# One megakernel, first part reshaped: the state-space rows of batch 0 spread by TensorE, the first feed-forward on ScalarE's Silu, and batch 1's scans ordered behind it

## What is computed

```
x += tanh(g_xattn[0]) * ssm(ctx, z=layernorm(x))      # state space, 512 channels, 16 states
x += tanh(g_ffn[0])   * ffn(layernorm(x))             # 512 -> 2048 -> 512, quantized weights
x += tanh(g_xattn[1]) * attention(layernorm(x), ctx)  # 16 heads of 128, keys/values from ctx
x += tanh(g_ffn[1])   * experts(layernorm(x))         # 4 experts

ssm:  u = silu(conv4(in_proj @ ctx) + conv_b);  dt, B, C = x_proj @ u     # 16 + 16 + 16 rows
      delta = softplus(dt_proj @ dt + dt_b)
      state[n] = exp(delta * A[n]) * state[n] + delta * u * B[n]          # for 16 states n
      y = sum_n state[n] * C[n] + D * u;   out = y * silu(z)
ffn:  bit_linear(silu(bit_linear(x, gate)) * bit_linear(x, val), out)
      # rows of x rounded to 8 bits by their maximum, weights to -1, 0, 1 by their mean
```

## Time and profile before

| what | value |
|---|---|
| time, median of 3 runs | 1866.79 us (1866.64 to 1868.19) |
| span of the profiled execution | 1867.3 us |
| TensorE busy | 1758.7 us (94%) |
| VectorE busy | 1317.8 us (71%) |
| ScalarE busy | 955.9 us (51%) |
| GpSimd busy | 663.5 us (36%) |

### The profile page before, as it was taken

One profiled execution on the slowest core, in us unless ns is written; L12 is line 12 of the kernel. 1 busy time (PEld: TensorE's weight loads), 2 busy tenths in 40 slices (PEclk: granted clock), 3 DMA queues, 4 the chain that ended last, 5 costly groups with the idle time before them and its releaser, 6 DMA issues.

```text
span 1867.3 us, 19387 instructions
## 1 busy us (share of the span) xinstructions
PE 1758.7 (94%) x6054; PEld 801.7 (43%) x6054; DVE 1317.8 (71%) x1919; ACT 955.9 (51%) x1904; POOL 663.5 (36%) x693
## 2 busy tenths in 40 slices
PE   8878769989999999999999999999999899999999
PEld 2323233434444344444444544444444344454543
DVE  3978877998998799889887989987643444422221
ACT  6867875656563555575456565564435233330100
POOL 1324522345472244456432464562123333310100
PEclk9989889999999899999999999999999999999999
DMA  8999933688771146697312589841112799846110
GB/s 267 260 289 291 300 109 98 173 211 215 189 195 46 48 102 155 160 266 196 102 31 70 129 199 234 212 109 62 41 47 78 215 301 256 246 141 241 68 51 28
DMA packets 163173, 300.30 MB, mean 161 GB/s; under 512 B 18936, under 2 KB 51704, under 8 KB 160128
## 3 DMA queue, kind: packets, MB, share of 16 engines
q1 hardware_dynamic: 145792, 236.14, 40.3%
q0 software_dynamic: 17280, 62.92, 17.5%
HBM read 177.64 MB, written 58.33 MB: 126 GB/s over the span
## 4 chain that ended last, share of the span: by engine, by line
PE 62%; DVE 18%; issue 6%; ACT 5%; DMA 5%; POOL 2%; SPq 2%; DVEq 0%; ACTq 0%; POOLq 0%
PE p L799 9%; PE p L776 8%; PE p L759 8%; PE p L810 8%; PE p L846 6%; DVE s_M L963 5%; PE p L652 4%; PE p L782 4%; PE p L861 3%; DVE s_M L958 2%; PE p L699 2%; DVE s_M L968 2%; PE p L733 2%; DMA s_bc<-bc_scratch 1%; PE p L738 1%
## 5 line engine op out<-in xcount | busy, mean ns | idle before, releaser
L963 DVE TENSOR_TENSOR_SCAN s_M<-s_M 128x1024 f32<-128x1024 f32 x128 | 296.8, 2319 | 7.8 <-ACT s_M L1218 5.3
L1106 DVE CUSTOM_DVE_ANT_0 s_U<-p,s_U 128x512 f32<-128x512 f32 x256 | 187.3, 745 | 162.8 <-PE p L776 161.5
L776 PE MATMUL p<-s_U 128*128 128x512 f32 x512 | 269.3, 614 | 5.6 <-DVE s_U L1106 2.8
L759 PE MATMUL p<-s_U 128*128 128x512 f32 x512 | 253.7, 604 | 4.7 <-DMA s_U<-in_Wq 2.1
L1445 POOL DMA_DIRECT2D s_u<-s_M x120 | 112.6, 938 | 391.5 <-DVE s_M L968 368.8
L1490 POOL TENSOR_SCALAR s_U<-s_U 128x512 f32<-128x512 f32 x256 | 229.4, 917 | 6.3
L810 PE MATMUL p<-s_U 128*128 128x512 f32 x512 | 224.0, 593 | 0.0
L799 PE MATMUL p<-s_U 128*128 128x512 f32 x472 | 213.6, 593 | 2.6 <-ACT s_U L1348 2.5
L1348 ACT COPY s_U<-p 128x512 f32<-128x512 f32 x196 | 105.3, 592 | 189.7 <-PE p L782 188.4
L1218 ACT ACTIVATE s_M<-s_dl,s_small 128x511 f32<-128x511 f32 x256 | 170.3, 718 | 40.3 <-DVE s_M L963 36.8
L1343 ACT ACTIVATE s_U<-s_U 128x512 f32<-128x512 f32 x256 | 181.6, 710 | 5.3
(11 more groups left out here) (171 smaller groups left out, 2364.3 us busy)
## 6 DMA issues: line engine op xcount, KB each, us to landing
s_u<-s_M POOLq DMA_DIRECT2D x120, 512.0 KB, 7.6
s_bc<-bc_scratch SPq DMA_DIRECT2D x128, 256.0 KB, 5.0
k_scratch<-s_U SPq DMA_DIRECT2D x16, 1024.0 KB, 9.4
v_scratch<-s_U SPq DMA_DIRECT2D x16, 1024.0 KB, 7.8
s_U<-in_Wq SPq DMA_DIRECT2D x64, 256.0 KB, 6.9
s_U<-k_scratch SPq DMA_DIRECT2D x64, 256.0 KB, 5.2
s_U<-rk_scratch SPq DMA_DIRECT2D x64, 256.0 KB, 5.5
s_U<-in_Wo SPq DMA_DIRECT2D x64, 256.0 KB, 4.5
```

Source lines behind the costliest of these rows:

```text
L759: ins = e.matmul(banks[bk][:], wqq[j % 2][:, k, :], axT[b % 2][:, k, :], start=(k == 0), stop=(k == 3))
L776: e.matmul(banks[bk][:], qT[j % 3][:, k * 128:(k + 1) * 128], kT[j % 2], start=True, stop=True).then_inc(S["a_s"], 1)
L963: e.tensor_tensor_scan(w, dA[i % 2], w, 0.0, ALU.mult, ALU.add).then_inc(S["m_s"], 1)
L1106: e.tensor_tensor_reduce(out=Pm[j % 2][:, k, :], in0=banks[ABANK[kind, j, k]][:], in1=rkb[j % 2], scale=rq[:, k:k + 1], scalar=-3.0e38, op ...
```

## The change

Four edits go together.

**1. B and C of batch 0 by TensorE.** The x_proj weights of batch 0 are laid out over 128 columns (dt, B, then B and C three times over), so one product of the same count gives copies of B and C on four groups of partitions. `split` turns these fp32 rows into three bf16 parts that add up to them (one ScalarE copy, four VectorE operations). `bc` i then makes, for state i, two bf16 matmuls with a 0/1 selector (built by GpSimd at the start) that put row B[i] and row C[i] on all 128 partitions, in PSUM banks 3/5 and 4/7. `mul` and `out` of batch 0 read PSUM. The 32 `spread` DMAs and the scratch write of batch 0 are gone. Batches 1 to 3 keep theirs.

**2. Softplus of batch 0** reads the `dt` products directly from four PSUM banks, with the bias, in four operations; the four Identity copies go.

**3. Silu in the feed-forward of batch 0.** ScalarE's Silu takes the place of Tanh, and the VectorE operation L1051 goes for batch 0 (16 times).

**4. Order.** Batch 1's softplus (and so its delta, decays and scans) must come after the last gate of batch 0's feed-forward. That feed-forward may enter before the last weight is quantized: its entry waits for the bias rows alone, its products for `put` 8, its first write to `h` and its output product for `put` 12.

```
-    order += [("dt", t) for t in range(4)] + [("sp", 0), ("soft", 0), ...
+    order += [("split", 0)] if b == 0 else []
+    order += [("dt", t) for t in range(4)] + ([("bc", 0), ("bc", 1)] if b == 0 else []) + [("sp", 0), ("soft", 0), ...
     for i in range(last):
         order += [("mul", i), ("scan", i), ("decay", i + ahead), ("out", i)] + ...
+        order += [("bc", i // 2 + 2)] if b == 0 and i % 2 and i < last - 2 else []
...
+        elif kind == "split":
+            part((kind, i), [("ACT", 0.6), ("DVE", 2.4)], ("xp", 3), free=[("xp", 0)])
+        elif kind == "bc":
+            part((kind, i), [("PE", 0.5)], ("out", 2 * i - 3) if i > 1 else ("split", 0))
-            part((kind, i), [("ACT", 3.3)], ("dt", 3))
+            part((kind, i), [("ACT", 3.6)], ("dt", 3), *([(0, "m", 3, 6)] if b == 1 else []), free=...)
...
-                part(name, [("DVE", 2.3)], ("m", t, k - 1), free=pair)
+                part(name, [("DVE", (2.3 if k % 4 == 3 else 1.5) if b else (1.9 if k % 4 == 3 else 0.8))], ("m", t, k - 1), *([] if b else [(0, "put", 2, 3)]), free=pair)
-                part(name, [("PE", 2.6), ("ACT", 0.7)], ("e", t, 2), take=pair)
+                part(name, [("PE", 2.6), ("ACT", 0.7)], ("e", t, 2), *([] if b else [(0, "put", 1, 3)]), take=pair)
-                part(name, [("DVE", 1.0), ("POOL", 1.1)], ("yt", 3), *([] if b else [(0, "put", 2, 3)]))
+                part(name, [("DVE", 1.0), ("POOL", 1.1)], ("yt", 3), *([] if b else [(0, "bias", 0, 2)]))
...
+                    elif kind == "bc":                                   # TensorE
+                        if i == 0:
+                            e.wait_ge(S["p_set"], 11)
+                            e.wait_ge(S["m_lo"], 1)
+                        if i >= 2:
+                            e.wait_ge(S["m_c"], 2 * i - 2)
+                        bk = BBANK[i % 2]
+                        vacant(bk)
+                        e.matmul(banks[bk][:], sel[:, i, :], parts, start=True, stop=True).then_inc(S["m_bc"], 1)
+                        freed[bk] = (S["m_s"], 2 * i + 2)
+                        bk = CBANK[i % 2]
+                        vacant(bk)
+                        e.matmul(banks[bk][:], sel[:, NS + i, :], parts, start=True, stop=True).then_inc(S["m_bc"], 1)
+                        freed[bk] = (S["m_c"], 2 * i + 2)
...
-                        if g == 0:                                       # VectorE, mul
-                            e.wait_ge(S[f"d_bc{n % 2}"], 32 * ((NS * b + n) // 2 + 1))
+                        if g == 0 and b == 0:
+                            e.wait_ge(S["m_bc"], 2 * n + 1)
...
+                    elif kind == "split":                                # VectorE
+                        e.tensor_tensor(rest[64:128, :], acc[64:128, :], parts[64:128, :], ALU.subtract)...
+                        e.tensor_copy(parts[64:128, :], rest[64:128, :])...
+                        e.tensor_tensor(rest[96:128, :], rest[96:128, :], parts[96:128, :], ALU.subtract)...
+                        e.tensor_copy(parts[96:128, :], rest[96:128, :]).then_inc(S["m_lo"], 1)
...
+                    elif kind == "sp" and b == 0:                        # ScalarE
+                        e.wait_ge(S["m_dt"], 4)
+                        for t in range(4):
+                            e.activation(dl[:, t, :], banks[LBANK[0, "dt", t]][:], ACT.Softplus, bias=dtb[:, t:t + 1])...
-                        e.activation(tt[i % 2], banks[...][:], ACT.Tanh, scale=qt[:, 12:13])...
+                        e.activation(tt[i % 2], banks[...][:], ACT.Tanh if b else ACT.Silu, scale=qt[:, 12:13])...
...
+                e.tensor_tensor(selr, identb[:, 32:64], identb[:, 64:96], ALU.add)...     # GpSimd, setup
+                e.tensor_tensor(selr, selr, identb[:, 96:128], ALU.add)...
+                e.tensor_copy(sel, selr.unsqueeze(2).to_broadcast([128, 2 * NS, 128]))...
-                    elif kind == "mul" and i % 2 == 0 and i < 2 * NS - 2:                 # SyncE
+                    elif kind == "mul" and b and i % 2 == 0 and i < 2 * NS - 2:
                         spread(i // 2 + 1)
```

More of the change, by code:

```diff
@@ L72, in mamba_order @@
     order += [(k, t) for t in range(4) for k in ("silu", "xp")] if b == 0 else [("silu", 4), ("xp", 4)]
-    order += [("dt", t) for t in range(4)] + [("sp", 0), ("soft", 0), ("soft", 1), ("init", 0), ("dv", 0)] + [("decay", i) for i in range(ahead)]
+    order += [("split", 0)] if b == 0 else []
+    order += [("dt", t) for t in range(4)] + ([("bc", 0), ("bc", 1)] if b == 0 else []) + [("sp", 0), ("soft", 0), ("soft", 1), ("init", 0), ("dv", 0)] + [("decay", i) for i in range(ahead)]
     last = 2 * NS - 2
@@ L229, in mamba @@
             last = i >= 3
-            part((kind, i), [("PE", 3.45 if b else 0.87)] + ([("ACT", 0.6)] if last else []), ("silu", i), take=[("xp", 0)] if i in (0, 4) else [], free=[("xp", 0)] if last else [])
+            part((kind, i), [("PE", 3.45 if b else 0.87)] + ([("ACT", 0.6)] if last else []), ("silu", i), take=[("xp", 0)] if i in (0, 4) else [], free=[("xp", 0)] if last and b else [])
+        elif kind == "split":
+            part((kind, i), [("ACT", 0.6), ("DVE", 2.4)], ("xp", 3), free=[("xp", 0)])
+        elif kind == "bc":
+            part((kind, i), [("PE", 0.5)], ("out", 2 * i - 3) if i > 1 else ("split", 0))
         elif kind == "dt":
-            part((kind, i), [("PE", 1.0), ("ACT", 0.7)], ("xp", 4 if b else 3), take=own, free=own)
+            part((kind, i), [("PE", 1.0)] + ([("ACT", 0.7)] if b else []), ("xp", 4 if b else 3), take=own, free=own if b else ())
         elif kind == "sp":
-            part((kind, i), [("ACT", 3.3)], ("dt", 3))
+            part((kind, i), [("ACT", 3.6)], ("dt", 3), *([(0, "m", 3, 6)] if b == 1 else []), free=[] if b else [("dt", t) for t in range(4)])
         elif kind == "soft":
@@ L243, in mamba @@
         elif kind == "mul":
-            part((kind, i), [("DVE", 1.25)], *([("out", i - NW)] if i >= NW else []))
+            part((kind, i), [("DVE", 1.25)], *([("out", i - NW)] if i >= NW else []), *([("bc", i // 2)] if b == 0 else []))
         elif kind == "scan":
@@ L680, in pe_ffn @@
                         product(t, g, ch, wqg).then_inc(S["f_g"], 1)
-                        freed[g] = (S["f_p"], i + 1)
+                        freed[g] = (S["f_p"], i - 15) if b else (S["f_th"], i + 1)
                         product(t, v, ch, wqv).then_inc(S["f_v"], 1)
@@ L695, in pe_ffn @@
                         e.wait_ge(S["f_hc"], 16 * b + 4 * t + 4)
+                        if t == 0 and b == 0:
+                            e.wait_ge(S["q_put"], 12)
                         bk = LBANK[b, "o", t]
@@ L967, in dve_mamba @@
                         e.wait_ge(S["m_s"], 32 * b + i + 1)
-                        e.tensor_tensor(w, w, rep(bcs[n % 2][:, 1, :], 2), ALU.mult).then_inc(S["m_c"], 1)
+                        if b == 0 and g == 0:
+                            e.wait_ge(S["m_bc"], 2 * n + 2)
+                        e.tensor_tensor(w, w, rep(bcs[n % 2][:, 1, :] if b else banks[CBANK[n % 2]][:], 2), ALU.mult).then_inc(S["m_c"], 1)
                     elif kind == "add":
```

96 lines of the change are left out of this document (71 added, 25 removed).

## The result

The changed kernel takes **1873.15 us** (median of 9 runs, 1868.44 to 1878.23) against 1866.64 us (9 runs) for the kernel before on the same chip: ratio 1.004, 95% interval 1.0026 to 1.0055, **slower by 0.4%**. I had forecast 1848, faster.

The account below looks back on a forecast made before the run. Bound: TensorE's work plus its idling and slow running before the first query product at 411.88 us. Terms 6.9 - 10 - 6 - 12 + 3 - 5 + 4 = -19 us gave 1848 us, range 1838 to 1860.

Parts of the forecast that it names:

- my +6.9: Front, TensorE: the 32 added selector matmuls for B and C cost +6.9 us.
- my +3: Front: TensorE newly waits on VectorE's read-outs before the selector matmuls, +3 us.
- R1: Rival: in the front TensorE and VectorE hold one another through the selector matmuls; slower, 1880 us; 13%.
- R5: Rival: TensorE's clock drops anew in gaps before the selector matmuls, to 0.85, costing 11 us; 1859 us; 8%.
- Weight waits: Front: fewer broadcasts loosen the DMA queues; half of TensorE's weight waits and slow clock goes, -10 us (0 to -20).
- The gate's wait: End of the front: TensorE's 14.5 us wait for batch 0's last gate shrinks, -12 us (0 to -16).
- The copies' waits: Front: a third of TensorE's 11.8 us behind ScalarE's PSUM copies and 5 us slow clock goes, -6 us.
- R2: Rival: DMA stays full and weights land as late, so only the gate wait shrinks; gain cancelled, 1867 us; 12%.
- Feed-forward of batch 0: Beside the key stream: it runs from about 240 to 325 us, hiding the 5.99 us wait for x, -5 us.
- By the first query batch 1 has done 13 or so steps instead of 10, so the attention loses nothing: Batch 1 beside the last keys: scans start near 320 us; the overlap costs +4 us, the attention nothing.
- R4: Rival: from 400 us on the reordered plan hurts the attention, through late scans by tens of us; 1885 us; 5%.

Follow-up runs that it names:

- bc_only: Kernel before plus only TensorE's B and C rows and softplus from PSUM for batch 0; Tanh and old order kept; 1853.65 us, ratio 0.9933.
- thin_steps: Changed kernel with VectorE handling only an eighth of the columns in batch 1's first ten steps; 1868.17 us, ratio 1.0005.
- order_only: Kernel before plus only Silu and the new order, batch 0 keeping its broadcasts; 1901.48 us, ratio 1.0197.
- hold_steps: early_wq with batch 1's eighth step and all later ones held behind head 1's transposed query; 1881.12 us, ratio 1.0084.
- tanh_gate: Changed kernel with Tanh and its VectorE operation back in batch 0's feed-forward, new order kept; 1878.33 us, ratio 1.0071.
- thin_adds: Changed kernel with batch 1's adding DMAs moving an eighth of their data; 1873.53 us, ratio 1.0049.
- early_wq: Changed kernel with the query weights of heads 0 and 1 loaded before the first feed-forward; 1870.47 us, ratio 1.0025.
- tanh_no_gate: Changed kernel with Tanh back and batch 1's softplus no longer held behind batch 0's last gate; 1856.25 us, ratio 0.9952.
- tanh_gate_tile1: Changed kernel with Tanh back and batch 1's softplus waiting for feed-forward tile 1 instead of tile 3; 1858.55 us, ratio 0.9965.
- bc_early_wq: bc_only with the query weights of heads 0 and 1 loaded before the first feed-forward; 1849.94 us, ratio 0.9897.
- silu_gate_tile1: Changed kernel, Silu kept, with batch 1's softplus waiting for feed-forward tile 1 instead of tile 3; 1877.18 us, ratio 1.0052.
- no_gate: Changed kernel, Silu kept, with batch 1's softplus no longer held behind batch 0's last gate; 1865.21 us, ratio 1.001.

## Why the prediction was wrong

**The front was right in sum, less so in its terms.** The first query moved by -18.7 us, against -19 forecast for all terms together. Of the terms: a pair of `bc` matmuls takes 0.44 us, 7 us together (my +6.9). No wait of TensorE's matmuls is named for them (my +3; their weight loads waited 1.1 us for VectorE in all), and none of VectorE's waits on broadcasts is left there. R1 did not happen, nor did R5, with a granted clock of 0.91 against 0.92. Weight waits fell by 13.5 us (10.6 + 5.0 to 2.1), I had taken -10 with the clock. The gate's wait fell by 14.5 (-12). The copies' waits did not fall by 6: my 11.8 us were two of five rows, and the five, 18.4 us, became 19.4. The longest of the new ones, 8.45 us, ends at 233.73 us, just ahead of where the wait for the gate had been, and it is none for a buffer: ScalarE makes the copy (L1369) in the middle of the last passes over the feed-forward's weights (L1258, L1263), with hardly a gap:

```profile
227.62 1.89 ACT L1263 ACTIVATE s_wq<-s_U 128x2048 fp8e4<-128x2048 f32 x1
229.42 1.99 ACT L1258 ACTIVATE s_U<-s_U,s_thr 128x2048 f32<-128x2048 f32 x1
231.31 1.89 ACT L1263 ACTIVATE s_wq<-s_x 128x2048 fp8e4<-128x2048 f32 x1
233.11 1.04 ACT L1369 COPY s_U<-p 128x512 f32<-128x512 f32 x2
```

R2, with the weights as late as before, did not happen either. The measured 1873 us lies between R2's 1867 and R1's 1880; that is chance, since neither mechanism is in the trace.

**The step that failed** is *Feed-forward of batch 0*, "It then runs from about 240 to 325 us", and with it the next one, "By the first query batch 1 has done 13 or so steps instead of 10, so the attention loses nothing". I took VectorE's load, 72 us, as the measure of the feed-forward's length. But its pieces stand in TensorE's queue between key products, and TensorE was full: 120.5 of 121.3 us between 240.0 and 361.3 us. (The 66 us for the 152 matmuls left are a slip too: the earlier trace rows give 0.487 us for one, 74 us.) The first gate product comes at 260.25 us and the last write to x at 361.24, so batch 1's first scan, which the order holds back, starts at 357.8 us and not near 320. By the first query batch 1 has started 6 steps, in bc_only 10.

The change did shorten the feed-forward. Its last write to x in the changed kernel, and then in bc_only, with Tanh and batch 1's early steps beside it:

```profile
361.24 0.74 DVE L1133 SCALAR_TENSOR_TENSOR s_x<-p,s_fq,s_x 128x512 f32<-128x512 f32 x1
```

```profile
384.55 0.72 DVE L1127 SCALAR_TENSOR_TENSOR s_x<-p,s_fq,s_x 128x512 f32<-128x512 f32 x1
```

These 23 us bought nothing, because the attention also needs the keys: TensorE is busy until 385 us in both kernels, and head 0's first query stands at 393.14 us in one and at 393.65 in the other. Two stretches of ten us in the changed kernel, and the same two of bc_only:

```profile
280.00:290.00 10.00, 10.00 (x42) 3.63 (x41) 1.26 (x3) 6.50 (x11) 0.00 (x0) 1.00 0.00 0
...
330.00:340.00 10.00, 10.00 (x54) 4.19 (x54) 3.23 (x5) 5.68 (x10) 0.00 (x0) 1.00 0.51 157
```

```profile
280.00:290.00 10.00, 10.00 (x43) 3.62 (x42) 5.84 (x11) 5.25 (x9) 0.00 (x0) 1.00 0.24 86
...
330.00:340.00 10.00, 10.00 (x42) 4.28 (x41) 9.86 (x9) 4.20 (x7) 5.40 (x2) 1.00 0.82 198
```

TensorE is busy for 10.00 of 10 us in all four. VectorE (the third busy figure) does 1.26 and 3.23 us in the changed kernel, 5.84 and 9.86 in bc_only, which has its scans there. The work I moved away had been free: the time to the first query was TensorE's, with it or without. The scans of batch 1 up to 470 us (durations min/median/max, first and last start), changed kernel and then bc_only:

```profile
L1011 DVE TENSOR_TENSOR_SCAN s_M<-s_M x17: 2289/2291/3705, 357.8 to 467.0; 128x1024 f32<-128x1024 f32 x17
```

```profile
L1011 DVE TENSOR_TENSOR_SCAN s_M<-s_M x21: 2281/2292/2579, 317.6 to 465.3; 128x1024 f32<-128x1024 f32 x21
```

They start 40 us later; 10 were started before VectorE's first score operation instead of 13 (my "instead of 10" was what the kernel before had reached by a later first query). A step takes VectorE 2.29 + 1.23 + 1.22 = 4.7 us, so the four missing ones by 470 us are 19 us. That this is the size of the loss proves nothing, since thin_steps took 36 us of such work away for 0.35%. Where the loss lies can be read: head 0 takes 54.2 us from its first query to the first mixing (393.14 to 447.33), in bc_only 38.6 (393.65 to 432.24). The difference, 15.6 us, is that of the spans, 15.1, and from the first mixing to the end both take 1420.8 us.

| kernel | ratio | scans by 470 us | first mixing | from there to the end | span |
|---|---|---|---|---|---|
| order_only | 1.0197 | 14 | 463.4 | 1432.5 | 1895.9 |
| hold_steps | 1.0084 | 16 | 426.2 | 1452.4 | 1878.5 |
| tanh_gate | 1.0071 | 16 | 439.3 | 1438.4 | 1877.7 |
| thin_adds | 1.0049 | 17 | 444.7 | 1425.4 | 1870.1 |
| changed | 1.004 | 17 | 447.3 | 1420.8 | 1868.1 |
| thin_steps | 1.0005 | 17 | 445.1 | 1427.2 | 1872.3 |
| early_wq | 1.0025 | 18 | 437.7 | 1423.0 | 1860.7 |
| bc_only | 0.9933 | 21 | 432.2 | 1420.8 | 1853.0 |
| tanh_no_gate | 0.9952 | 22 | 434.9 | 1418.3 | 1853.2 |
| tanh_gate_tile1 | 0.9965 | 22 | 438.8 | 1416.4 | 1855.2 |
| bc_early_wq | 0.9897 | 22 | 429.2 | 1418.5 | 1847.7 |

Spans are of one profiled execution each and can lie off the median, early_wq's 8 us under it. Two kernels with Silu between Exps are not in the table: silu_gate_tile1 has 22 scans, its first mixing at 449.0 us and a span of 1868.6 us, no_gate 24, 437.9 and 1859.3, with some 20 table loads more than the changed kernel. For the others both ratio and span go by and large with the number of steps done, better than with the first mixing. The last part takes 1416 to 1427 us, but for the three kernels with the fewest steps, where it takes 1432 to 1452: hold_steps and tanh_gate mix early and pay at batch 1's feed-forward (10.2 + 5.2, and 8.1 us of waiting for VectorE). That is R4's mechanism ("If batch 1's later scans delayed its feed-forward past the last head of batch 0, the price would be tens of us"), which I gave 5% because of the 13 steps. In the changed kernel itself no such wait is there (none over 1.7 us between 500 and 900 us): it pays at the handover, for which R4 had allowed 10 us either way inside my range.

**Shown**: that edits 3 and 4 together cost 20 us; that the order alone costs 22 us with Tanh and 6 us with Silu; that with Tanh the loss goes when batch 1's steps may start earlier; that in the changed kernel's trace it lies between the first query and the first mixing; that changing the order of the queues there (hold_steps) does not remove it; and that neither DMA load nor the late weights of heads 0 and 1 nor VectorE's own time is its main part. **Argued**: that the late steps cost what they do because they hold three in-order queues among head 0's pieces; and that Silu's cost without the order is its table loads. **Open**: why the same order costs 37 us without edits 1 and 2 (its first scan is at 376.4 us, 19 us later still, which fits but was not tried by itself); why silu_gate_tile1 is slower than no_gate; and whether Silu with its Exps grouped in time would pay.

## What to carry to other kernels

Before moving work off an engine "to make room" for a phase, ask which engine sets that phase: where TensorE is full, other engines' work beside it can be free. Taking it away may end the phase sooner, here by 23 us, and still gain nothing, if what comes next waits for TensorE's other work. Work that is moved past a handover can cost more than its own engine's time, because it stands in every in-order queue it passes; count how many steps are done at the handover before and after, with the phase's length taken from the engine that bounds it. And test a bundle of edits part by part: here two gained 0.7% and the other two lost 1.1%.

## What the runs showed of the hardware

- A change of ScalarE's function between Silu and Exp costs 1.30 us from the load's start to the next operation's start in the rows above; with Tanh among the Exps the whole kernel has 25 loads (tanh_no_gate), with Silu 43 (no_gate).
- The granted clock fell to its lower level in a single wait: after 8.08 us of idling in the changed kernel eight fp32 products of 512 columns took 6.12 us at a mean granted clock of 0.60, and the next such eight, 10 us later, 3.70 us at 1.00.
- Two bf16 products with a 0/1 selector for each state, 32 in all, replaced 32 broadcast DMAs; a pair takes 0.44 us of TensorE. VectorE waited for one of them once, 1.8 us; no wait of TensorE's matmuls is named for them, only 1.1 us of their weight loads' for VectorE.
